# A mixture-of-experts layer whose first product is written transposed, with its weights fetched from DRAM for each slot

## The reference

```
x = x + attn_a(norm(x)); x = x + ffn(norm(x)); x = x + attn_b(norm(x)); x = x + ffn(norm(x))
ffn(x):                                   # x as 2048 rows of 128
  probs = softmax(x @ w_gate + b_gate)    # 8 experts
  route_p, route_idx = max(probs), argmax(probs)
  h = relu(x @ W1[e] + b1[e])             # W1[e]: 128 x 512, b1[e]: 512
  y = h @ W2[e] + b2[e]                   # W2[e]: 512 x 128
  out = y[route_idx] * route_p
```

## Time and profile before

| | |
|---|---|
| time, median of three executions | 582.98 us (582.77 to 583.08) |
| span of the profiled execution, first to last instruction | 579.5 us |
| PE busy | 435.6 us (75%) |
| DVE, ACT, POOL busy | 340.7, 219.0, 203.6 us |
| the two slot stages of the FFN in the trace | 196.5 to 258.2 us, and 488.7 to 551.8 us |

### The profile page before, as it was taken

One profiled execution on the slowest core, in us unless ns is written; L12 is line 12 of the kernel. 1 busy time (PEld: TensorE's weight loads), 2 busy tenths in 40 slices (PEclk: granted clock), 3 DMA queues, 4 the chain that ended last, 5 costly groups with the idle time before them and its releaser, 6 DMA issues.

```text
span 579.5 us, 14261 instructions
## 1 busy us (share of the span) xinstructions
PE 435.6 (75%) x4663; PEld 328.6 (57%) x4679; DVE 340.7 (59%) x1067; ACT 219.0 (38%) x507; POOL 203.6 (35%) x300
## 2 busy tenths in 40 slices
PE   3667899999976299982656899899878862999900
PEld 2545677777765167771334667666666652677700
DVE  4545567677876544444865675667777674455412
ACT  1445655556450022220133667656655410122200
POOL 5032333344453300007865156435712442000054
PEclk9978999999995599995557999999999975899965
DMA  8999200000000011111100000000000001111123
GB/s 262 358 344 292 61 3 3 10 10 9 9 12 16 29 42 52 54 41 41 36 1 2 1 2 2 1 0 0 1 1 6 24 24 32 38 55 54 42 67 91
DMA packets 40895, 30.89 MB, mean 53 GB/s; under 512 B 3344, under 2 KB 37008, under 8 KB 40592
## 3 DMA queue, kind: packets, MB, share of 16 engines
q1 hardware_dynamic: 32176, 23.06, 12.9%
q0 software_dynamic: 2048, 4.20, 2.4%
q10 hardware_dynamic: 6624, 3.02, 1.8%
HBM read 15.26 MB, written 15.01 MB: 52 GB/s over the span
## 4 chain that ended last, share of the span: by engine, by line
PE 54%; DVE 18%; issue 8%; ACT 7%; POOL 6%; DMA 4%; SPq 1%; ACTq 0%; DVEq 0%; another core or an unknown queue 0%; POOLq 0%
PE S L1324 8%; PE bank L1337 7%; PE S L1248 5%; POOL yg L1052 4%; PE S L1330 4%; DVE nmax L497 3%; ACT E L918 3%; PE bank L1203 3%; PE S L1414 2%; PE bank L1367 2%; PE S L1415 2%; PE bank L1427 2%; PE bank L1164 2%; PE bank L1390 2%; PE bank L1225 2%
## 5 line engine op out<-in xcount | busy, mean ns | idle before, releaser
L836 ACT ACTIVATE E<-S,nmax 128x256 f32<-128x256 f32 x128 | 58.9, 472 | 67.9 <-DVE nmax L497 67.9
L1052 POOL DMA_INDIRECT yg<-slots,pos x32 | 30.8, 963 | 140.6 <-DMA slots<-yo 132.1
L1248 PE MATMUL S<-QT,KT 128*128 128x256 f32 x256 | 67.2, 408 | 0.8 <-DVE Va L386 0.5
L880 ACT ACTIVATE hT<-S 128x512 f32<-128x512 f32 x46 | 27.5, 597 | 105.9 <-PE S L1330 105.9
L1013 POOL TENSOR_TENSOR vs<-Va,rden 128x512 f32<-128x512 f32 x32 | 33.3, 1041 | 88.5 <-DVE rden L526 72.3
L497 DVE TENSOR_REDUCE nmax<-S 128x4 f32<-128x1024 f32 x32 | 39.1, 1221 | 31.2 <-PE S L1248 30.6
L918 ACT ACTIVATE E<-S 128x1536 f32<-128x1536 f32 x32 | 46.4, 1450 | 25.4 <-PE S L1418 25.4
L1248 PEld LDWEIGHTS S<-QT,KT 128*128 128x128 f32 x256 | 49.1, 202 | 9.2 <-DVE Va L386 0.6
L1324 PE MATMUL S<-W,xgT 128*128 x92 | 52.3, 652 | 0.0
L684 DVE TENSOR_REDUCE nm<-bank 128x2 f32<-128x512 f32 x64 | 41.1, 683 | 15.7 <-remote 10.6
L1337 PE MATMUL bank<-W,hT 128*128 x368 | 48.5, 275 | 0.0
(11 more groups left out here) (171 smaller groups left out, 1011.1 us busy)
## 6 DMA issues: line engine op xcount, KB each, us to landing
slots<-zeros SPq DMA_DIRECT2D x1, 8640.0 KB, 37.9
xg<-slots SPq DMA_DIRECT2D x46, 64.0 KB, 1.7
slots<-yo ACTq DMA_DIRECT2D x46, 64.0 KB, 1.6
W<-in_L_ffn_W SPq DMA_DIRECT2D x1, 2048.0 KB, 10.0
b<-in_L_ffn_b SPq DMA_DIRECT2D x1, 2048.0 KB, 20.3
x<-in_L_attn_a_x SPq DMA_DIRECT2D x4, 256.0 KB, 3.6
yg<-in_select SPq DMA_DIRECT2D x1, 1024.0 KB, 7.6
out<-x SPq DMA_DIRECT2D x8, 128.0 KB, 2.2
```

What stands on the lines that cost most here:

```text
L836: last = act.activation(E[:, hp, h, c, :], S[hp % 2][:, h, c * T:(c + 1) * T], ACT.Exp, bias=nmax[:, hp, k:k + 1], accum_out=den[:, hp, k: ...
L1052: pool.indirect_dma_start(out=yg[:, t, :], out_offset=None, in_=xs_dram, in_offset=bass.IndirectOffsetOnAxis(pos[:, t:t + 1], 0)).then_inc ...
L1248: last = pe.matmul(S[hp % 2][:, h, c * T:(c + 1) * T], KT[:, p, h, hp, 4 * c:4 * c + 4, :], QT[:, p, :, hp * RT:(hp + 1) * RT], start=True ...
```

## The change

W1 is no longer held whole. SP fetches the 256 KB of the slot's expert from DRAM for each slot, into a ring of three buffers (`NW = 3`). In SP's program the fetch of W1 for slot s+2 stands behind the fetch of the tokens of slot s, and it waits until the first product of slot s-1 is done, because that product was the last to read its buffer. PE makes the hidden block transposed from the start: four products with a 128x128 piece of W1 stationary and the transposed tokens moving. b1 is then one value per partition, so ACT adds it and applies relu to two of the four pieces in one instruction each, and DVE does the same for the other two. The four transposes between the layers go, the second product of a slot moves one step nearer to its first, and each engine's last step goes. b1 is loaded as 4096 single values instead of a broadcast. A few semaphores are shared or renamed.

The diff, with the renaming of semaphores and the lower count of the `w_loaded` waits left out:

```diff
**Rows 3.**DIFF**Rows 3.**
```

More of the change, by code:

```diff
@@ L34 @@
 MC = MLP // P
+NW = 3
 SLOTS = NT + NE - 1
@@ L108, in build @@
         OT = sb("OT", [P, 2, 2, 4, RT])
-        W1 = sb("W1", [D, NE, MLP])
+        W1 = sb("W1", [D, NW, MLP])
         W2 = sb("W2", [P, NE, MC, D])
-        b1 = sb("b1", [P, NE, MLP])
+        b1 = sb("b1", [P, NE, MC])
         b2 = sb("b2", [P, NE, D])
@@ L211, in build @@
             ffn.append({k: sem(f"f{n}_{k}") for k in
-                        ("logits", "chain", "chain1", "chain2", "exp", "counts", "rank", "totals", "pos", "go",
+                        ("logits", "chain", "chain1", "chain2", "exp", "counts", "rank", "totals", "pos",
                          "table", "scat0", "scat1",
-                         "in0", "in1", "xt", "xgT", "h", "hb", "ht", "hT", "y", "yo",
+                         "in0", "in1", "w0", "w1", "w2", "xt", "xgT", "h", "hTa", "hTd", "y", "yo",
                          "out0", "out1", "x")})
@@ L226, in build @@
         slots_zero = sem("slots_zero")
+        dve_go = sem("dve_go")
+        pool_go = sem("pool_go")
         block = ctx.enter_context(nc.Block())
@@ L299, in b_parts, with hidden, slot_steps @@
             chain.wait()
-        def slot_steps(eng, step, last):
+        def hidden(par, c):
+            return S4[:, 2 * par + c // 2, (c % 2) * P:(c % 2 + 1) * P]
+        def slot_steps(eng, step, last, first=-1):
             held = None
-            for s in range(-1, 3):
-                held = step(s, s % 2, held)
+            for s in range(first, 3):
+                held = step(s, s % 6, s // NW, held)
             each = 6
@@ L310, in slot_steps @@
                 for i in range(each):
-                    held = step(k * each + (3 + i), (3 + i) % 2, held)
+                    held = step(k * each + (3 + i), (3 + i) % 6, k * (each // NW) + (3 + i) // NW, held)
             held = None
             for s in range(SLOTS - 2, last + 1):
-                held = step(s, s % 2, held)
+                held = step(s, s % 6, s // NW, held)
         x_view = x_in.rearrange("b (u p) d -> p (b u) d", p=P)
@@ L345, in ffn_loads, with weights, step @@
                 f = ffn[n]
+                sp.wait_ge(f["table"], 1)
+                def weights(s, m):
+                    e = sp.value_load(expert[0:1, bass.ds(s, 1)], min_val=0, max_val=NE - 1)
+                    waits(sp, f["h"], s - (NW - 1))
+                    sp.dma_start(W1[:, m % NW, :], W1_in[bass.ds(e, 1), :, :].squeeze(0)).then_inc(f[f"w{m % NW}"], 16)
+                def step(s, m, w, held):
+                    at = sp.value_load(row[0:1, bass.ds(s, 1)], min_val=0, max_val=ROWS - P)
+                    waits(sp, f["xt"], s - 1)
+                    sp.dma_start(xg[:, m % 2, :], xs_dram[bass.ds(at, P), :]).then_inc(f[f"in{m % 2}"], 16)
+                    if live(s + 2):
+                        weights(s + 2, m + 2)
+                weights(0, 0)
+                weights(1, 1)
                 sp.wait_ge(f["scat0"], 16 * NT // 2)
                 sp.wait_ge(f["scat1"], 16 * NT // 2)
[L348 to L360, removed]
+                slot_steps(sp, step, SLOTS - 1, 0)
             ffn_loads(0)
@@ L605, in ffn_tiles, with step @@
                 dve.wait_ge(f["table"], 1)
-                def step(s, par, held):
+                def step(s, m, w, held):
+                    par, before = m % 2, held
+                    e = None
+                    if live(s - 1) and before is None:
+                        before = dve.value_load(expert[0:1, bass.ds(s - 1, 1)], min_val=0, max_val=NE - 1)
                     if live(s):
@@ L615, in step @@
                         dve.wait_ge(f["h"], s + 1)
[L616 to L621, removed]
+                        waits(dve, f["y"], s - 1)
+                        for c in range(MC // 2, MC):
+                            last = dve.tensor_scalar(hT[:, par, c, :], hidden(par, c),
+                                                     b1[:, bass.ds(e, 1), c:c + 1].squeeze(1), 0.0, ALU.add, ALU.max)
+                        last.then_inc(f["hTd"], 1)
+                    if live(s - 1):
+                        dve.wait_ge(f["y"], s)
                         if isinstance(s, int):
-                            waits(dve, f[f"out{par}"], 16 * ((s - 2) // 2))
+                            waits(dve, f[f"out{1 - par}"], 16 * ((s - 1) // 2))
                         else:
-                            dve.wait_ge(f[f"out{par}"], (s - 2 - par) * 8)
-                        dve.tensor_tensor(yo[:, par, :], pb[1 + par][:, 0:D], b2[:, bass.ds(e2, 1), :].squeeze(1),
+                            dve.wait_ge(f[f"out{1 - par}"], (s - 1 - (1 - par)) * 8)
+                        dve.tensor_tensor(yo[:, 1 - par, :], pb[2 - par][:, 0:D], b2[:, bass.ds(before, 1), :].squeeze(1),
                                           ALU.add).then_inc(f["yo"], 1)
-                slot_steps(dve, step, SLOTS + 1)
+                    return e
+                slot_steps(dve, step, SLOTS)
             def ffn_add(n, c):
@@ L872, in ffn_tiles, with step @@
                 f = ffn[n]
[L874 to L887, removed]
+                def step(s, m, w, held):
+                    par = m % 2
+                    if live(s):
+                        e = act.value_load(expert[0:1, bass.ds(s, 1)], min_val=0, max_val=NE - 1)
+                    if live(s - 2):
+                        at = act.value_load(row[0:1, bass.ds(s - 2, 1)], min_val=0, max_val=ROWS - P)
+                    if live(s):
+                        act.wait_ge(f["h"], s + 1)
+                        waits(act, f["y"], s - 1)
+                        for c in range(MC // 2):
+                            last = act.activation(hT[:, par, c, :], hidden(par, c), ACT.Relu,
+                                                  bias=b1[:, bass.ds(e, 1), c:c + 1].squeeze(1))
+                        last.then_inc(f["hTa"], 1)
+                    if live(s - 2):
+                        act.wait_ge(f["yo"], s - 1)
+                        act.dma_start(xs_dram[bass.ds(at, P), :], yo[:, par, :]).then_inc(f[f"out{par}"], 16)
+                act.wait_ge(f["table"], 1)
+                slot_steps(act, step, SLOTS + 1)
             norm_out(1, 6, 0, pb[1])
@@ L1306, in ffn_tiles, with step @@
                 pe.wait_ge(f["table"], 1)
[L1308 to L1311, removed]
+                def step(s, m, w, held):
+                    par, before = m % 2, held
+                    e = None
+                    if live(s - 1) and before is None:
+                        before = pe.value_load(expert[0:1, bass.ds(s - 1, 1)], min_val=0, max_val=NE - 1)
                     if live(s):
@@ L1321, in step @@
                     if live(s):
+                        pe.wait_ge(f[f"w{m % NW}"], w * 16 + 16)
                         pe.wait_ge(f["xgT"], s + 1)
-                        waits(pe, f["hb"], s - 1)
-                        pe.matmul(S4[:, par, :], xgT[:, par, :], W1[:, bass.ds(e, 1), :].squeeze(1), start=True, stop=True
-                                  ).then_inc(f["h"], 1)
+                        waits(pe, f["hTa"], s - 1)
+                        waits(pe, f["hTd"], s - 1)
+                        for c in range(MC):
+                            last = pe.matmul(hidden(par, c), W1[:, m % NW, c * P:(c + 1) * P], xgT[:, par, :],
+                                             start=True, stop=True)
+                        last.then_inc(f["h"], 1)
                     if live(s - 1):
-                        pe.wait_ge(f["hb"], s)
-                        waits(pe, f["hT"], s - 2)
+                        pe.wait_ge(f["hTa"], s)
+                        pe.wait_ge(f["hTd"], s)
+                        waits(pe, f["yo"], s - 2)
                         for c in range(MC):
[L1330 to L1338, removed]
+                            last = pe.matmul(pb[2 - par][:, 0:D], hT[:, 1 - par, c, :],
+                                             W2[:, bass.ds(before, 1), c, :].squeeze(1), start=(c == 0), stop=(c == MC - 1))
                         last.then_inc(f["y"], 1)
-                    return e, before
-                slot_steps(pe, step, SLOTS + 1)
+                    return e
+                slot_steps(pe, step, SLOTS)
             ffn_tiles(0)
```

14 lines of the change are left out of this document (6 added, 8 removed).

## The result

The changed kernel takes 728.74 us (median of four, 727.47 to 731.23) against 582.88 for the kernel before: 1.2513 times its time, 95% interval 1.2471 to 1.2554, or 146 us more. The forecast was 707 with a range of 663 to 730, so the time lies 1.3 us inside the range's upper edge. The direction and the mechanism were right; the size was 22 us short.

A forecast was written before the change was run, and what follows sets the result against it. PE was taken as the bound, 2.41 us a slot. 40 x (5.35 - 2.41) = 117.6, + 5 for stage starts + 2 for ends = 124.6 us on 582.98 gave 707.6, forecast as 707, range 663 to 730.

The forecast's parts named there:

- SP's queue, the step that decides: Slot stages: tokens s+1 queue behind W1's wait for first product s-1; closed loop, 4.55 to 5.55 us against 2.41, 40 slots.
- SP's steps (items 1, 2 and 6): In each loop turn: SP's waking and address 0.20 us, W1 issue to token issue 1.12, register arithmetic 0.08.
- The landing (item 3): In each loop turn: tokens land 1.75 us after issue, W1's 0.88 us transfer just clear; bounds nothing and 0.9 more.
- the full collision (+0.9): Rival: W1's transfer delays each token landing by 0.9 us, 743 us in all; sign: landing over 2.2 us; chance 0.07.
- Transpose and first product (items 4 and 5): PE's part of each loop turn: 0.30 and 1.06 us at full clock, 0.48 and 1.88 at half.
- Which clock: PE in the slot stages: mostly half clock, a fifth of slots at full, so 5.35 us a slot; chance 0.45.
- neither full nor half clock throughout: Two rivals for PE's clock in the slot stages: 2.4 GHz kept, 669 us, chance 0.22; half throughout, 721 us, chance 0.20.
- Start of a stage: Before the first product, extra W1 issues by SP: +3.6 us in the first FFN, +1.3 in the second, together +5.
- End of a stage: After slot 20's first product: -1.9 to +3.5 us per FFN against 7.4 before; +1 taken, +2 for both.
- Start of the kernel: Loads: W1 gone, b1's 4096 small pieces take some 17 us; zeros +3 us later, 20 us of cover, cost nothing.
- PE, DVE and ACT: Work per slot: PE 1.89 us at full clock, 0.41 less; DVE's operations 0.29 each, ACT's 0.31; new waits cost nothing.
- The faster rival: SP isn't held up by W1's wait; a slot takes 2.1 us as PE, DVE and ACT allow, 571 us; chance 0.05.

The follow-up runs named there:

- the other order: Changed kernel, still three buffers, but SP asks for slot s's tokens and then W1 of slot s instead of slot s+2: 582.36 us, 1.0002 times before.
- the small fetch: Changed kernel with each slot's W1 fetch moving 64 of 512 columns (32 KB for 256 KB), same issues and waits: 694.71 us, 1.192 times before.
- the other half: Kernel before, with its own compute and transposes, plus the ring of three for W1 and the changed order of SP's issues: 714.62 us, 1.2252 times before.

## Why the prediction was right, and where it was short

- *SP's queue, the step that decides*: right, and shown by the runs with six buffers and with the other order. The number of turns, 40, is the number of SP's waits. The other signs that I had named came too: the token issue starts 1.33 us after the first product has ended, and PE waits 2.5 us a turn for the tokens (47.6 us in the 19 turns of the first FFN), at the upper end of the 1.8 to 2.5 that I gave.
- *SP's steps (items 1, 2 and 6)*: right. 1.40 us were put in, with 0.04 for PE's waking 1.44. One turn of the chain has 231.27 to 232.60, 1.33 us, for SP; the loop's turns, which are not in the sum, lengthen some (2.2 us in place of 1.33 in the turn from 243.89 to 251.03, where SP branches). The mean of everything that is not landing, transpose or product is 1.49.
- *The landing (item 3)*: this is the step that failed in size. The sum has 1.75 us; measured were 2.4 in the median and 2.42 in the mean of the chain's 38 turns, 1.8 to 2.8 in single ones. That is 0.67 x 40 = 27 us, more than the whole error; the small fetch gave it back. "It has just left the engines when they need them" was wrong. The sum let the 0.88 us of transfer end within the 1.12 us between the two issues. The trace after the W1 issue at 231.43 has the engines busy from 0.8 to 2.4 us after it, and the tokens, issued at 232.60, come into that (columns as above):

```profile
231.80:232.20 0.40, 0.40 (x4) 0.40 (x4) 0.23 (x1) 0.22 (x1) 0.00 (x0) 0.50 0.00 0
232.20:232.60 0.40, 0.40 (x4) 0.34 (x3) 0.00 (x0) 0.00 (x0) 0.00 (x0) 0.81 0.90 97
232.60:233.00 0.40, 0.13 (x2) 0.00 (x0) 0.12 (x1) 0.00 (x0) 0.00 (x0) 1.00 0.78 92
233.00:233.40 0.40, 0.00 (x0) 0.00 (x0) 0.17 (x1) 0.00 (x0) 0.00 (x0) 1.00 0.67 246
233.40:233.80 0.40, 0.00 (x0) 0.00 (x0) 0.00 (x0) 0.00 (x0) 0.00 (x0) 1.00 0.93 323
233.80:234.20 0.40, 0.00 (x0) 0.00 (x0) 0.00 (x0) 0.00 (x0) 0.00 (x0) 1.00 0.47 106
```

In the six turns in which SP branches, the W1 issue is 1.3 to 2.0 us ahead of the tokens' instead of 1.17, and those tokens land after 1.8 to 2.3 us, 2.0 in the mean. ACT's write-back, issued at 231.67, is in the same stretch; the small fetch left it there and the landing was short, so it doesn't lengthen the landing by itself; its part beside W1 wasn't tested. I had the full collision (+0.9) as a rival at 0.07, as if it were all or nothing; two thirds of it is the usual case. Of the signs that I had named, the landing over 2.2 us spoke for that rival, and it came.
- *Transpose and first product (items 4 and 5)*: right at either level: 0.33 + 1.05 at full clock, 0.47 + 1.8 at half (0.30 + 1.06 and 0.48 + 1.88 in the sum).
- *Which clock*: right, though the fifth at full clock was a guess. With it the sum has 1.72 us for the first product and 0.44 for the transpose; the means are 1.67 and 0.40. Of the rivals, neither full nor half clock throughout held. The granted clock of 0.67 and 0.71 is higher than the 0.6 of a fifth, but it counts the stall too, in which, as in the rows above, it can be 1.00 while PE does nothing. The Trainium skill, "TensorE: Matmul & The Clock Gate", section "HAM oscillation — how this bites in real kernels", has the bursts between DMA waits fall back to half; the waits in its example are longer than those here. The trace agrees in part: of the 38 first products in the turns of the chain, 26 took over 1.7 us, as at half clock, seven took 1.0 to 1.2, full clock, and five lay between.
- *A turn together*: 5.35 + 0.67 (landing) + 0.05 (SP and waking) - 0.05 (first product) - 0.04 (transpose) = 5.98, the measured turn.
- *Start of a stage*: +3.6 was forecast for the first FFN. From the table's last instruction to the end of the first product it is 207.13 - 197.30 = 9.8 against 202.65 - 196.52 = 6.1: +3.7. In the second it is 573.20 - 563.57 = 9.6 against 494.66 - 487.72 = 6.9: +2.7, where +1.3 was forecast. The table is done only 1 us before the scatter lands (487.72 and 488.71 in the kernel before), so the scatter hides 1.0 us of the 2.2 that the two W1 issues take, where I had it hide all; and the tokens land after 2.2 us instead of 1.8.
- *End of a stage*: 7.4 before; 334.42 - 327.60 = 6.8 after in the first FFN; 550.76 - 543.21 = 7.6 and 698.07 - 691.02 = 7.0 in the second. That is -0.6 and -0.5, within the bounds and better than the +1 taken.
- *The range*: that the time fell inside it is partly luck. The landing alone would have put the sum at 734, outside; the ends of the two stages gave 3 us back.
- *Start of the kernel*: nothing, as forecast. The zeros are issued at 22.6 and land 33.7 later, at 56.3, six us earlier than before. With W1 gone and b1 still broadcast, in the run of the other half, they land at 56.5, so the single values of b1 cost about what the broadcast did, not the 10 us more that I gave them. At 197 us the two kernels are within 1 us of each other.
- *PE, DVE and ACT*: PE's 1.89 us a slot was right, as the version with POOL's copies shows. DVE's and ACT's new operations took 0.347 and 0.363 us, not 0.29 and 0.31, and are not in the chain of the 19 turns, so they cost nothing there.
- *The faster rival*: it was rightly put last, since SP was held up. But its price was wrong: once SP isn't held up, the time is 582 or 586 us, not the 571 I gave it. I had PE, DVE and ACT as limits and left out SP itself, though its 1.12 us an issue stood in my own sum. With W1 copied by POOL it is 572.

## What to carry to other kernels

An engine here runs its program in order, so a wait belongs to everything behind it. When a fetch is added to a queue, find what stands behind its wait, and how late that may be; sort the issues by the time at which their waits end, or add buffers until the wait is always over (here either gave back over 140 us). Then count the issues themselves: two per slot with register loads were 2.34 us, a bound of its own. And when a large block is fetched just ahead of a small one that something waits for, put part of its transfer into the small one's landing (here 0.67 us, with 1.17 us between the two issues).

## What was new on the hardware

- A 256 KB fetch issued 1.17 us ahead on the same queue lengthened a 64 KB landing from 1.7 to 2.4 us; with the fetch on POOL's queue the landing was 2.6. So it isn't the order within one queue alone; the profile has the packets of both queues on the same 16 engines.
- Useless work on PE made the kernel faster by 14 us, by raising its granted clock from 0.67 to 0.96 on a path that passed through PE for 2 of 6 us. Four of them, with the small fetch, took 11 us off where ten had taken off none.
- POOL copied 128x512 float32 within SBUF in 0.61 us; its operation with two inputs of that size takes 1.04.
